# Where ScalarE empties the scores of unit 1: ahead of a group's exponentials, or behind the first of them

## The reference, cut to what matters

```python
dots = jnp.einsum('bhid,bhjd->bhij', q, k) * SCALE
dots = jnp.einsum('bhij,hk->bkij', dots, pre_proj)
causal = jnp.triu(jnp.ones((n, j), bool), j - n + 1)
dots = jnp.where(causal, NEG_INF, dots)
topk_vals = jax.lax.top_k(dots, K)[0]          # K = 64
thresh = topk_vals[..., -1:]
dots = jnp.where(dots < thresh, NEG_INF, dots)
attn = jax.nn.softmax(dots, axis=-1)
out = jnp.einsum('bhij,bhjd->bhid', attn, v)
```

## Time and profile before

| | |
|---|---|
| median of 3 runs | 2672.58 us (2666.22 to 2674.03) |
| the profiled execution, its own time | 2676.88 us |
| its span, first to last instruction | 2674.8 us |
| mean granted TensorE clock | 0.904 |
| PE busy | 2203.2 us, 82% |
| DVE busy | 2150.8 us, 80% |
| ACT busy | 1575.8 us, 59% |
| exponentials of the 64 groups (L630) | 358.6 to 2425.7 us |

### The profile page before, as it was taken

One profiled execution on the slowest core, in us unless ns is written; L12 is line 12 of the kernel. 1 busy time (PEld: TensorE's weight loads), 2 busy tenths in 40 slices (PEclk: granted clock), 3 DMA queues, 4 the chain that ended last, 5 costly groups with the idle time before them and its releaser, 6 DMA issues.

```text
span 2674.8 us, 34886 instructions
## 1 busy us (share of the span) xinstructions
PE 2203.2 (82%) x10182; PEld 1298.6 (49%) x10182; DVE 2150.8 (80%) x9008; ACT 1575.8 (59%) x2342; POOL 553.5 (21%) x427
## 2 busy tenths in 40 slices
PE   6599656777778758888899889999994899988997
PEld 3466333434444434455555545555552555545665
DVE  1512599999999989999898898998898989987445
ACT  1122134556666637777777777887773878785222
POOL 0000002222223213222223313322311233231000
PEclk9599667789889979999999999999997999988999
DMA  2000000000000000000000000000000000002000
GB/s 67 1 0 0 16 1 1 1 1 1 1 1 1 1 0 1 1 1 1 1 1 1 1 1 1 1 1 1 1 1 0 1 1 1 1 3 70 1 1 16
DMA packets 18072, 13.65 MB, mean 5 GB/s; under 512 B 6975, under 2 KB 15817, under 8 KB 17865
## 3 DMA queue, kind: packets, MB, share of 16 engines
q1 hardware_dynamic: 13824, 8.92, 1.3%
q10 hardware_dynamic: 4038, 2.37, 0.3%
HBM read 9.19 MB, written 2.10 MB: 4 GB/s over the span
## 4 chain that ended last, share of the span: by engine, by line
PE 46%; DVE 36%; ACT 10%; issue 4%; POOL 2%; DVEq 2%; ACTq 1%; POOLq 0%
PE bank L935 10%; DVE cand L1238 9%; PE bank L919 7%; PE bank L903 7%; DVE F L1309 5%; ACT R L630 5%; PE bank L1007 5%; PE bank L920 3%; DVE W L1268 2%; PE bank L1015 2%; ACT R L580 2%; DVE W L1267 2%; DVE R L1296 2%; DVE r L1298 2%; DVE r L1293 2%
## 5 line engine op out<-in xcount | busy, mean ns | idle before, releaser
L903 PE MATMUL bank<-hT,qT 128*128 128x512 f32 (+3 forms) x1280 | 599.6, 606 | 211.3 <-ACT R L580 118.7
L1238 DVE MAX8 cand<-R 128x8 f32<-128x12 f32 (+15 forms) x4096 | 673.9, 224 | 3.8 <-ACT R L580 3.7
L935 PE MATMUL bank<-WP,Y 128*128 128x512 f32 x1088 | 582.2, 628 | 0.5 <-ACT WP L637 0.2
L447 POOL TENSOR_TENSOR X<-R,X 128x144 f32<-128x144 f32 (+15 forms) x64 | 163.9, 2561 | 1843.0 <-ACT X L623 1843.0
L903 PEld LDWEIGHTS bank<-hT,qT 128*128 128x128 f32 x1280 | 246.9, 212 | 482.7 <-issue 202.6
L919 PE MATMUL bank<-ident,R 128*128 128x128 f32 x2176 | 436.1, 283 | 23.6 <-ACT R L630 15.9
L630 ACT ACTIVATE R<-R,negm 128x144 f32<-128x144 f32 (+15 forms) x256 | 309.6, 1211 | 183.3 <-DVEq L1393 183.3
L920 PE MATMUL bank<-nidentb,F 128*128 128x128 bf16 x2176 | 404.4, 222 | 0.0
L637 ACT ACTIVATE WP<-bank 128x512 f32<-128x512 f32 x544 | 321.3, 594 | 119.7 <-PE bank L920 109.1
L919 PEld LDWEIGHTS bank<-ident,R 128*128 128x128 f32 x2176 | 311.6, 143 | 153.4 <-issue 92.1
L580 ACT ACTIVATE R<-bank 128x1024 f32<-128x1024 f32 (+7 forms) x384 | 290.8, 772 | 141.9 <-PE bank L903 73.8
(11 more groups left out here) (244 smaller groups left out, 2753.4 us busy)
## 6 DMA issues: line engine op xcount, KB each, us to landing
R<-in_L_attn_Wkv ACTq DMA_DIRECT2D x2, 512.0 KB, 8.7
out<-X SPq DMA_DIRECT2D x1, 1024.0 KB, 5.1
R<-in_L_ffn_gate_w SPq DMA_DIRECT2D x1, 1024.0 KB, 8.0
R<-in_L_ffn_up_w SPq DMA_DIRECT2D x1, 1024.0 KB, 11.5
out<-X SPq DMA_DIRECT2D x4, 256.0 KB, 2.3
R<-in_L_attn_Wq ACTq DMA_DIRECT2D x1, 512.0 KB, 6.6
WP<-in_L_attn_Wo ACTq DMA_DIRECT2D x1, 512.0 KB, 10.7
R<-in_L_ffn_wi SPq DMA_DIRECT2D x1, 256.0 KB
```

The source lines that it names most:

```text
L447: pool.tensor_tensor(OV[i - 2][:, 0:n], S[:, k % NS, i, 0:n], OV[i - 2][:, 0:n], ALU.subtract)\
L903: last = pe.matmul(to, qT[:, k % 2, i, :], hT[:, a:b], start=True, stop=b < n, skip_group_check=True)
L935: pe.matmul(bank[6], Y[:, j, :], PT[:, (blocks_before(k) + j) % 4, :], start=(j == 0), stop=(j == k // 4))\
L1238: mark(dve.max(cand[:, :, c, i], lists(S[:, k % NS, i, 0:n], n, c)))
```

## The change

`late_from` becomes smaller by one, so one slot less is drained early:

```diff
             def late_from(k):
 
-                return 1 + 2 * slots(k // 4)
+                return 2 * slots(k // 4)
```

## The result

The changed kernel takes 2744.38 us (2740.57 to 2751.84, 4 runs), beside 2673.31 (2666.22 to 2674.1, 4 runs) of the kernel before in the same comparison: a ratio of 1.0291, 95% interval 1.026 to 1.0323, or 71 us more. The profiled execution took 2745.25 us. Forecast were 2754, that is 81 us more, in a range of 2710 to 2800.

What follows compares the result with a forecast made beforehand. DVE alone sets the pace to about 1000 us; afterwards a chain through ACT's exponentials and drains, PE's unit 3 fill and DVE's threshold binds. 64 - 9 + 8 + 18 = +81 us gives about 2754 us, range 2710 to 2800.

Steps and rivals of the forecast that it cites:

- Unit 3's fill one exponential and one drain later, passed on whole from group 30: PE's fill of unit 3 in groups 30 to 61 starts an exponential and a drain of 1b later: +64 us.
- What comes back in the last groups: Exponential 0 starts sooner where ACT itself is late, groups 57 to 61 and slightly 53, 54, 56: -9 us.
- The small groups, +8: One-slot groups: same shift, partly absorbed by slack; +8 us for groups 20 to 29, nothing below; bounds nothing to 18.
- The clock, +18: More PE idle lowers TensorE's granted clock by one and a half hundredths over 1270 us: +18 us, bounds nothing to 51.
- the sum to about 115 us: By the skill's rule on PSUM cycling, the clock term would be nearer its upper end, the sum about 115 us.
- about 50 us up: Sign: DVE's wait at L1356 for ACT's counts rises about 50 us, and POOL's share of its waits too.
- hardly changed: Sign: ACT's idle time for DVE's release (L1393), 183.3 us ahead of exponential 0 before, stays nearly the same.
- the other two signs that the prediction is wrong: Unit 3's end to DVE's threshold becomes shorter than 18.77 us in tile 8; clock moves by more than 0.04.
- Mostly absorbed: Rival: slack in POOL's or ACT's order absorbs 1.3 us per large group, 42 us in all: 2712 us; chance 0.13.
- no difference: Rival: what follows the exponentials has as much room as ACT's 183 us idle: 2672 us; smaller loss or none 0.06.
- faster: Rival: PE's transposes of unit 0 end last, so the 9 us come through and the 64 not: 2663 us; chance 0.04.
- the clock gives way everywhere: Rival: groups 30 to 61 fill unit 3 at the low clock, small groups pass all 18 us: 2797 us; chance 0.15.

## Why the prediction was right, point by point

**Unit 3's fill one exponential and one drain later, passed on whole from group 30.** Right in kind and in size: 64 - 9 = 55 us forecast, 55.9 measured between the releases of groups 30 and 62. The term itself, the fill's start behind exponential 0, is 65.7 us in all against 64. Group 41 shows the 1.76 us, group 33 the unchanged 18.78 us behind the fill. Undoing the push with 1b left where it is gives the time back, and the push the other way gains until another end takes over; in both a part of the time is the clock's.

**What comes back in the last groups.** Right: 1.8 us in group 58, and 8.8 us over groups 30 to 61 against 9.

**The small groups, +8.** The mechanism was right, the size too small: 18.7 us in the profile, 20 in the kernel that changes them alone. My bounds, nothing to 18, were for groups 20 to 29 alone: these are 12.5 us longer, and groups 0 to 19, which I had put at nothing, 6.2. I took groups below 20 to be free because DVE waited for nobody, which says that there is slack and not how much; and I read the slack from DVE's wait for counts, while the first to run out is POOL's subtraction (L1293). In groups 20 to 29 I had the shift right, 18 us in all, and even had too little of it absorbed. What I had left out is that the fill of unit 3 falls to the low clock there as well. It is 8.6 us longer in all, no fill of the ten runs wholly at the high level any more (six did), and 18.0 + 8.6 us of lateness, less 14.1 absorbed, make the 12.5.

**The clock, +18.** This term was mis-sized: unit 3's fills took about 1 us more, and their start holds at most 2 more. The clock of the large groups did fall, 0.96 to 0.94, near what I took. The wrong step is the price: I multiplied the fall of the mean clock by all of PE's time there, as if each hundredth stood on the chain. The fills of unit 3, which do, lost nearly as much to the low level before: 129.6 us in all before, 130.7 after. What fell is the clock ahead of them, where PE waits for ACT anyway, so the 28.6 us of full speed lost there don't reach the fills. That 3b waits for q's drain hides nothing new, for it stands in the same order in both kernels; in group 41 q's drain ends at 1513.88, and 3b's fill begins at 1514.95, right behind 3a's:

```profile
1513.28 0.60 ACT L569 ACTIVATE qT<-bank 128x512 f32<-128x512 f32 x1
```

The rule of the Trainium skill that I cited (TensorE: Matmul & The Clock Gate, "A second HAM failure mode: psum-queue depth-cycling") holds as far as the clock falling with more idle stretches goes; that it would bring the sum to about 115 us did not come true.

**The signs I named.** DVE's wait at L1356 "about 50 us up" was wrong by name: it rose by 8, and the two waits for POOL by 65. ACT idle for the release "hardly changed" was wrong: 73 us more; ACT reaches exponential 0 with one drain less, and the release itself comes later. PE's wait at L903 for L580 grew by only 14 us, in 84 places instead of 89. I had named the wrong line: q's fill (L885) stands first behind the drain of 2a, and its wait for L580 grew by 55. From exponential 0 to the end of unit 3's fill I had named 1.3 us more in group 33, 2.1 in group 45 and 2.7 in group 59; measured are 2.84, 1.98 and 2.71. The first is out because the fill of group 33 changed from the high to the low clock. L1238 waits for L580 once in the whole run, 3.7 us, and did so before, so DVE doesn't wait for unit 1's lists, as forecast; nor did the other two signs that the prediction is wrong appear.

**The rivals.** "Mostly absorbed", "no difference" and "faster" are out by the interval. Of "the clock gives way everywhere" the part on the small groups came true, with the fills there at the low level and 19 us passed on; the part on the large groups did not.

The two errors, 11 too little in the small groups and 17 too much for the clock of the large ones, partly cancel, and that is luck: the clock was priced where it cost nothing and left out where it cost. 81 was forecast, 71 measured, and a second measurement gives 80; with the clock term at 1 us and the small groups as forecast it would have been 64.

## What to carry to other kernels

A drain that is moved by one place in an in-order queue moves all the drains behind it, and the one that another engine's fill waits for decides: count the long instructions that now stand ahead of that one, not the length of the drain moved. Whether the lateness is paid shows before any change, by two neighbouring groups of which one happened to be late, and the end from which both keep the same distance. Idle time of an engine ahead of its own long work (ACT's 183 us ahead of the exponentials) is the place to put short work that another engine waits for; one more drain there won 36 us (a part of them by the clock), two more lost 21 of them. A lower mean clock is not a price: ask on which instructions the low level falls, and whether anything waits for their end.

## What the runs showed of the hardware

Two added matmuls per group with useless results, some 2 us of PE's time in a wait, made the kernel before 19 us faster. They raised the granted clock of the large groups from 0.96 to 0.98 and brought 29 of 32 fills of unit 3 wholly to the high level, from 15. In the changed kernel three of them raised it from 0.94 to 0.96 and shortened the fills by 30 us, but they ran past the drain that PE waits for and delayed the same fills by 22, which left 8 in the profiled executions and 9 in the medians. So what such work wins depends on its ending before the wait does.

Two kernels with a granted clock of 0.96 and 0.94 in their large groups had fills of unit 3 of nearly the same total length, 129.6 and 130.7 us: the mean says little about the clock of the instructions that count.
